# A transformer mixer layer: the maxima of the scores taken three at a time, and the norm of a later chunk moved among the global heads

## What is computed

```
xn = (x - mean) / sqrt(var + 1e-5)
q, k, v = split(xn @ w_qkv + b_qkv)                 # 16 heads of 16
w = softmax(where(mask, -inf, q k^T / 4))           # heads 0-3: causal; heads 4-15: causal, 64 keys back
attention = concat(w v) @ w_out + b_out

xV = einsum(Q, V); yW = cumsum(einsum(K, W))        # Q, K: projections of xn; 8 experts of 64
weights = softmax(gelu(Q @ r1 + b1) @ r2 + b2 + expert_bias)
branch = (einsum(xV * yW * weights, U) + weights @ b) / (position + 1)
experts = (branch(forward) + alpha * branch(inverse)) @ W_O
```

## Time and profile before

| what | us |
|---|---|
| median of 3 runs (1558.54 to 1561.29) | 1560.65 |
| the profiled execution's own time | 1558.8 |
| its span in the profile | 1557.1 |
| TensorE busy (matmuls) | 1468.7 |
| VectorE busy | 882.2 |
| ScalarE busy | 795.6 |
| GpSimd busy | 444.0 |

### The profile page before, as it was taken

One profiled execution on the slowest core, in us unless ns is written; L12 is line 12 of the kernel. 1 busy time (PEld: TensorE's weight loads), 2 busy tenths in 40 slices (PEclk: granted clock), 3 DMA queues, 4 the chain that ended last, 5 costly groups with the idle time before them and its releaser, 6 DMA issues.

```text
span 1557.1 us, 36810 instructions
## 1 busy us (share of the span) xinstructions
PE 1468.7 (94%) x15153; PEld 1082.1 (69%) x15153; DVE 882.2 (57%) x1935; ACT 795.6 (51%) x1432; POOL 444.0 (29%) x471
## 2 busy tenths in 40 slices
PE   5999999999999999999999999999999999999997
PEld 4577775867758676676757767576775867667674
DVE  6675672747637484474836567274762748547361
ACT  3446446463554536555374644646356453654534
POOL 1042331414224231332404233141322413133230
PEclk9999999999999999999999999999999999999999
DMA  8423416153241615316052341615325162531610
GB/s 220 83 71 98 122 35 160 50 124 109 77 125 32 171 61 117 99 44 175 31 137 82 100 131 37 149 61 118 115 69 134 32 162 69 115 100 39 167 31 15
DMA packets 153787, 150.56 MB, mean 97 GB/s; under 512 B 28467, under 2 KB 136884, under 8 KB 153572
## 3 DMA queue, kind: packets, MB, share of 16 engines
q1 hardware_dynamic: 153620, 148.22, 36.1%
HBM read 106.98 MB, written 34.87 MB: 91 GB/s over the span
## 4 chain that ended last, share of the span: by engine, by line
PE 74%; DVE 12%; ACT 7%; issue 4%; POOL 1%; DMA 1%; SPq 0%; DVEq 0%; ACTq 0%; POOLq 0%
PE PS L639 33%; PE PS L760 9%; PE PS L841 4%; PE PS L904 3%; PE PS L873 3%; PE PS L794 3%; PE PS L814 3%; PE PS L820 3%; DVE prod L1334 3%; ACT HE L1085 3%; PE PS L855 3%; PE PS L780 2%; PE PS L885 2%; PE PS L959 2%; DVE block_peak L1261 2%
## 5 line engine op out<-in xcount | busy, mean ns | idle before, releaser
L1506 POOL TENSOR_TENSOR PL<-prod,PH 128x512 fp32r<-128x512 f32 x128 | 164.1, 1282 | 264.7 <-ACT PH L1050 264.2
L639 PE MATMUL PS<-XH,WH 128*128 128x512 f32 x512 | 220.5, 431 | 4.4 <-DVE XL L1201 1.9
L1050 ACT ACTIVATE PH<-prod 128x512 fp32r<-128x512 f32 x128 | 80.9, 632 | 264.0 <-DVE prod L1334 264.0
L639 PE MATMUL PS<-XH,WL 128*128 128x512 f32 x512 | 203.8, 398 | 0.0
L639 PE MATMUL PS<-XL,WH 128*128 128x512 f32 x512 | 203.4, 397 | 0.0
L1261 DVE TENSOR_REDUCE block_peak<-PS 128x4 f32<-128x512 f32 x288 | 188.8, 683 | 8.6 <-PE PS L794 8.6
L1501 POOL TENSOR_TENSOR prod<-prod,rest 128x512 f32<-128x512 f32 x96 | 123.6, 1289 | 243.4 <-ACT prod L1040 144.8
L1494 POOL TENSOR_SCALAR_AFFINE_SELECT HE<-HE 128x256 f32<-128x256 f32 x128 | 50.7, 409 | 478.5 <-ACT HE L1085 475.9
L1085 ACT ACTIVATE HE<-PS 128x512 f32<-128x512 f32 (+1 forms) x320 | 159.7, 552 | 24.9 <-PE PS L855 22.6
L1254 DVE TENSOR_REDUCE peak<-PS 128x4 f32<-128x512 f32 x192 | 124.6, 683 | 35.8 <-PE PS L780 35.5
L1040 ACT ACTIVATE prod<-PS 128x512 f32<-128x512 f32 x128 | 76.2, 595 | 131.2 <-PE PS L639 131.2
(11 more groups left out here) (193 smaller groups left out, 3163.5 us busy)
## 6 DMA issues: line engine op xcount, KB each, us to landing
parts_d<-area SPq DMA_DIRECT2D x32, 768.0 KB, 5.1
area<-parts_d SPq DMA_DIRECT2D x128, 192.0 KB, 8.4
rest<-weights_d SPq DMA_DIRECT2D x192, 128.0 KB, 2.9
area<-parts_d SPq DMA_DIRECT2D x32, 576.0 KB, 8.5
tok<-in_L_attn_x_dram SPq DMA_DIRECT2D x16, 512.0 KB, 6.3
xt<-in_L_attn_x_dram SPq DMA_DIRECT2D x16, 512.0 KB, 4.0
wide<-weights_d SPq DMA_DIRECT2D x64, 128.0 KB, 3.0
out_dram<-xt SPq DMA_DIRECT2D x16, 512.0 KB, 3.7
```

The costliest lines, as they stand in the source:

```text
L639: ins = e.matmul(ps, a, b, start=first and k == 0, stop=last and k == n - 1, skip_group_check=True)
L1050: e.activation(PH[:, h, :], prod[:, j % 3, :], ACT.Copy).then_inc(phi)
L1506: e.tensor_tensor(PL[:, j % 2, :], prod[:, j % 3, :], PH[:, j % 2, :].bitcast(F32), ALU.subtract).then_inc(plo)
```

## The change

The maxima are returned in triples rather than pairs. Each triple comes in two lists: the masks (seeds) that its maxima need, and the maxima with what is attached to them (`found`, `rows`, in chunk 0 the norm). A new function `weave_peaks` runs a group of experts, then the masks of the triple to come, then, when it is due, that triple. The masks of a triple are thus planned behind the next group of experts after the former triple. The norm is taken out of the maxima except in chunk 0 (which norms chunk 1), and its nine pieces for chunk ch + 2 are attached to the groups of the global heads of chunk ch, from one third of them on.

```
+    PEAKS = 3
...
+    def weave_peaks(main, peaks):
+
+        done, masks = 0, []
+        for n, group in enumerate(main):
+            run(group + masks)
+            masks = []
+            upto = -(-len(peaks) * (n + 1) // len(main))
+            for m in range(done, upto):
+                run(masks + peaks[m][1])
+                masks = peaks[m + 1][0] if m + 1 < len(peaks) else []
             done = upto
...
+    def add_norm(ch, order):
+
+        at_ = len(order) // 3
+        for n in range(len(NORM)):
+            order[at_ + n * (len(order) - at_) // len(NORM)].append((add, "norm", ch, n))
+
     def peak_groups(ch):
...
+        masks = [[] for _ in order + gpeaks]
         for n, ((stage, *key),) in enumerate(order + gpeaks):
             if stage is add_lpeak and n > 2:
-                order[n - 2].append((add_seed, key[-1], "lpeak", *key[:-1]))
+                masks[n].append((add_seed, key[-1], "lpeak", *key[:-1]))
             elif stage is add_gpeak and key[2] == c * T + key[1]:
-                (order + gpeaks)[n - 2].append((add_seed, key[-1], "gpeak", *key[:-1]))
+                masks[n].append((add_seed, key[-1], "gpeak", *key[:-1]))
...
-        if ch + 1 < CHUNKS:
-            at_ = len(order) // 3
-            step = (len(order) - at_) // len(NORM)
-            for n in range(len(NORM)):
-                order[at_ + n * step].append((add, "norm", ch + 1, n))
-        return [order[n] + (order[n + 1] if n + 1 < len(order) else []) for n in range(0, len(order), 2)]
+        if ch == 0:
+            add_norm(1, order)
+        join = lambda groups: [stage for group in groups for stage in group]
+        return [(join(masks[n:n + PEAKS]), join(order[n:n + PEAKS])) for n in range(0, len(order), PEAKS)]
...
-        weave(experts[:split], peaks)
+        weave_peaks(experts[:split], peaks)
...
             order = order[1:]
+            if ch + 2 < CHUNKS:
+                add_norm(ch + 2, order)
```

More of the change, by code:

```diff
@@ L215, in weave @@
             done = upto
+    def weave_peaks(main, peaks):
[7 more added lines that the diff above has]
+                masks = peaks[m + 1][0] if m + 1 < len(peaks) else []
+            done = upto
     def run(group):
```

## The result

The changed kernel takes 1587.49 us (median of 4 runs, 1587.1 to 1592.64) against 1560.97 us: a ratio of 1.0178, with a 95% interval from 1.0157 to 1.0200. It is slower by 24 to 31 us. The profiled execution took 1592.64 us, with a span of 1590.9; it is the longest of the four, at a mean granted clock of 0.990, where the other three have 0.993 or 0.994.

A forecast was written before the change was run, and what follows sets the result against it. TensorE was taken to set the time, with VectorE close to its limit in odd chunks. Added 55.3 us less 37.3 off gave net +18.0, so about 1578 us for the median; range 1564 to 1588.

The forecast's parts named there:

- (1): Phase of experts: the norm leaves chunks 1 to 14, waits struck out, 3.4 us off per odd chunk, 0.57 per even.
- (6): Global heads: the moved norm makes `cinv` 0.6 us late in even chunks, `cparts` about 0.1; 0.7 us added in all.
- (3): Behind `c` of expert 1, a triple waits for three late masks: 2.78 us lost per odd chunk, 2.41 per even.
- (4): Odd chunks, behind `x` of expert 3: a triple waits for its masks, 1.85 us lost per chunk, 13.0 in all.
- (5): Odd chunks: twice a triple follows a `mix` with the product still queued, third bank 0.2 us late; 2.8 in all.
- (2): Fewer changes between expert and maxima matmuls: 0.7 us off per odd chunk, 0.5 per even, 8.9 in all.
- has the same chain behind product 0: Chunk 0, counted with the even chunks: late masks behind product 0 lose 2.41 us.
- The last chunk: No norm to lose there; its late masks and the like waits it already has cancel, to within 2 us.
- 1 (changes of matmul kind dear): Faster: 72 fewer changes of matmul kind at 0.5 us each give 36 us; time 1551, chance 0.10.
- 2 (losses made good later in the chunk): No difference: TensorE gets back about 1.1 us a chunk in waits later in the chunk; time 1561, chance 0.06.
- 3 gave 1588: Slower: in even global heads norm operations and GpSimd selects hold each other up, 10.5 us more; 1588, chance 0.10.

The follow-up runs named there:

- early masks: The change with the next triple's masks planned right behind a triple, ahead of the next expert group: 1530.21 us, ratio 0.9804 to the kernel before.
- The norm alone: The kernel before, pairs and masks as they were, with only the norm of chunks 2 to 15 moved among the global heads: 1546.92 us, ratio 0.9911.
- second profile: The change itself run once more, unaltered: 1591.71 us, ratio 1.0190 to the kernel before.

## Why the prediction was wrong

The direction was right and the mechanism stood in the sum: ScalarE's order and the masks behind its copies. The measured time, 1.0178 times that of before, is 1588.4 us on the basis of the 1560.65 that I started from, just over the upper end of my range. The change cost about 27 us where my sum gave 18.

**Steady chunks: right, in odd ones partly by luck.** For chunks that the clock left alone, terms (1) to (6) sum to +0.93 us in an odd chunk (2.78 + 1.85 + 0.4 - 3.4 - 0.7) and +1.44 in an even one (2.41 + 0.1 - 0.57 - 0.5). Measured from the chunks' starts and ends they are +0.87 and +1.47. The run with early masks parts the terms taken off from those added. In an odd phase the terms taken off come to 43.04 - 39.58 = 3.46 us, where I had 4.1, and the late masks add 43.89 - 39.58 = 4.31, where I had 5.03: two errors of about 0.7 that cancel. In an even phase it is 1.17 for 1.07 and 2.32 for 2.41.

- (3) From the last start of `c` in chunk 3 (375.91) and its step of 0.24, `c` ends at 376.15 and the triple at 379.69: 3.54 us, where I had 3.56. (4) The same count behind `x` gives 385.27 + 1.38 - 383.94 = 2.71, where I had 2.63. With early masks the two triples are over 0.88 and 0.91 us behind, where I took 0.78 off.
- (5) Nothing of it shows: of the 3.69 us that TensorE idles in chunk 3, 3.58 are in the triples behind that `c` and that `x`.
- (1) The norm alone is worth 1.84 and 0.27 us, where I had 2.2 and within 0.57; striking out all waits of the odd chunk was right because new ones took their place.
- (2) Triples for pairs, with early masks, bring 1.62 and 0.91 us. Of that 0.90 and 0.36 are TensorE's idle time, the old waits that I had struck out in (1); its busy time falls by 0.72 and 0.55, where I had 0.7 and 0.5 for the changes.
- (6) The norm among the global heads takes 6.8 us where I had 6.4, and costs 0.33 us in an even chunk where I had 0.1.

**The step that failed: chunk 0 "has the same chain behind product 0".** I counted it as an even chunk, +1.44. It cost 9.3 us in the first profile. Its product 0 waits for GpSimd's first `weigh`, and that for the first gate rows from memory; the masks wait behind PH of that product. VectorE's timeline after, at that product:

```profile
90.78 0.69 DVE L1354 TENSOR_TENSOR prod<-PS,prod 128x512 f32<-128x512 f32 x1 [2.26 <-POOL prod L1521]
```

and TensorE's, at the triple:

```profile
92.68 1.45 PE L800 MATMUL PS<-area 96*64 96x128 bf16 x24 [3.30 <-ACT PS L1076]
```

The wait is 3.30 us (2.29 in the second profile), and another, where the norm stays among its maxima, 1.09. I had even credited chunk 0 with 0.57 for a norm that it keeps; an even chunk that keeps its norm beside triples loses another 2.7 us. With the waits filled and one fall left, chunk 0 still cost 7.9 us in all; in pairs 1.8. A fall of the same mean clock made chunk 1 of the second profile 1.3 us longer, so by this estimate I was some 5 us short there from waits.

**The term that was missing: the clock.** I priced a wait at its own length. In this kernel a wait of 1 to 3 us can also let the granted clock fall to 1.2 GHz behind it. I gave it no term. It is worth 7.4 us over the run. With the change's waits filled the ratio is 1.0144, and with chunk 0 in pairs it is 1.0149; on my basis both are below 1585 us, so either error alone would have left the time inside my range. Before the change no chunk from 0 to 14 shows a fall, with waits of up to 0.97 us in the odd chunks.

**The last chunk** I took to cancel within 2 us; it cost 3.3 us in the first profile at a clock of 0.92 and 1.4 us with the waits filled.

**The rivals.** 1 (changes of matmul kind dear) falls: six changes fewer in an odd chunk and three in an even one bring 0.72 and 0.55 us of busy time, 0.12 and 0.18 us each, and with the idle time of (2) 0.27 and 0.30, where the rival needs 0.37; and the late masks took more. 2 (losses made good later in the chunk) falls: local and global heads take what they took before, to within 0.05 us in odd chunks. 3 gave 1588, almost the measured time, for a wrong reason: the wait of the weighted values for selects is unchanged, and the scaling moved behind `cout` gives back the whole 0.33 us. It is the norm that is held up: three of its operations beside the four selects of chunk 4 last 0.40, 0.33 and 0.36 us (549.22 to 550.02 in the rows above). These lines of the waits of after and of before show the selects:

```profile
PE PS L893 <- POOL HE L1514: 8.8, 26, 0.7
```

```profile
PE PS L873 <- POOL HE L1494: 8.8, 26, 0.7
```

The Trainium skill (SBUF — State Buffer, "SBUF: two separate sides") says that, where both need the ports that VectorE and GpSimd share, whichever starts first has them for its whole instruction and the other blocks. These operations agree: each starts while a select runs and lasts no longer than a select's 0.41 us, where beside GpSimd's products one of them took up to 1.13. With no GpSimd instruction beside them the same operations take 0.15 to 0.17 us, so the three are some 0.6 us longer in all. That covers the 0.4 us by which the norm exceeds my 6.4, and with it the 0.23 us by which (6) was short; no run takes it away by itself.

**What stays open.** Which of the equal waits lets the clock fall: two profiles of the changed kernel showed falls in chunk 2, or in 13 and 14, besides chunks 0, 1 and 15. The length of a wait does not decide alone either: 2.27 us in chunk 0 in pairs had no fall behind it, 0.75 us in chunk 15 with early masks had one. That waits make the falls is shown; what picks the chunk was not tried.

## What to carry to other kernels

Where one engine prepares something for another and has time to spare, plan it ahead of its other work for the next group. Behind that work, the other engine may have to wait for it: here the position of 13 small copies per chunk (nine masks for lpeaks, four for gpeaks) decided between 1.8% slower and 2% faster. When the same mechanism repeats in many stages, look separately at the first stage, where the inputs of the chain are not ready yet. And a wait on TensorE can cost more than its length, as here in some chunks: look at the granted clock of the stretch behind it.

## What the hardware showed that I had not expected

TensorE's granted clock fell to its lower level behind waits of about 1 to 3 us (once 0.75) in an otherwise busy kernel, and did not do so in every chunk with the same waits (chunks 3 to 12 of the change were spared in both profiles). Matmuls whose results nobody reads, put into those waits, kept it up in the phases of all chunks but the first and gave 7.4 us back.
